# A fused tokenizer, attention and routed-expert kernel: the chunks routed in five groups in place of four

## What is computed

```python
h = h + attn(layernorm(h))      # decayed running sums over the tokens, times mix_w.T, plus mix_b
x = layernorm(h).reshape(-1, 128)
logits = x @ Wg                                  # 8 experts
topw, topi = top_k(logits, 2); topw = softmax(topw)
gu = einsum('nd,edh->enh', x, Wgu) + bgu         # 2 x 256 columns for each expert
eo = einsum('enh,ehd->end', silu(g) * u, Wd) + bd
h = h + sum over the two experts chosen of topw * eo
```

## Time and profile before

| what | before |
|---|---|
| median of 3 runs | 802.29 us (799.72 to 802.66) |
| profiled execution | 798.29 us |
| its span, first to last instruction | 796.5 us |
| busy: PE, POOL, DVE, ACT | 609.1, 475.6, 427.2, 264.0 us |
| mean granted clock of TensorE | 0.825 of 2.4 GHz |
| scatters and gathers (POOL indirect DMAs) | 180 and 180 |
| tiles | 114 |

### The profile page before, as it was taken

How to read it: one execution, slowest core, us unless ns; L and a number is a source line. 1 busy time by engine, 2 the same in 40 slices (tenths; PEclk the granted TensorE clock), 3 DMA queues, 4 the chain that set the end, 5 groups by cost and what they waited for, 6 DMA issues and landing times. The chain is left out here.

```text
span 796.5 us, 12820 instructions
## 1 busy us (share of the span) xinstructions
PE 609.1 (76%) x3335; PEld 521.8 (66%) x3335; DVE 427.2 (54%) x1724; ACT 264.0 (33%) x690; POOL 475.6 (60%) x504
## 2 busy tenths in 40 slices
PE   3692557756998987999989897999898869999000
PEld 2592457755887875788768676888776658887000
DVE  4668787764564565656456664555445323545122
ACT  2611312221533333544324441533433324443000
POOL 5613377634777653566767664677777567750774
PEclk9796557665997877889869987999999979999555
DMA  7197010204565443655646555677767578984221
GB/s 146 44 312 200 2 28 27 78 14 153 171 191 148 144 143 108 199 154 179 192 134 204 150 169 193 180 210 218 218 177 247 155 240 262 279 255 153 75 79 59
DMA packets 84598, 125.23 MB, mean 157 GB/s; under 512 B 15044, under 2 KB 57792, under 8 KB 84526
## 3 DMA queue, kind: packets, MB, share of 16 engines
q1 hardware_dynamic: 72526, 101.66, 42.0%
q0 software_dynamic: 11520, 22.35, 9.9%
q10 hardware_dynamic: 480, 0.41, 0.4%
HBM read 84.25 MB, written 43.25 MB: 160 GB/s over the span
## 5 line engine op out<-in xcount | busy, mean ns | idle before, releaser
L627 PE MATMUL gu<-space,wts 128*128 128x256 f32 x912 | 247.0, 410 | 3.0 <-DVE space L1511 3.0
L1511 DVE SCALAR_TENSOR_TENSOR space<-gu,wts,space 128x256 f32<-128x256 f32 x228 | 108.3, 481 | 237.2 <-ACT space L955 185.5
L1085 POOL DMA_INDIRECT gat<-ybuf,ypos x180 | 177.1, 984 | 94.4 <-issue 56.0
L1071 POOL DMA_INDIRECT xbuf<-x,pos x180 | 183.0, 1017 | 68.2 <-issue 61.8
L955 ACT ACTIVATE space<-gu,wts 128x256 f32<-128x256 f32 x228 | 109.0, 479 | 304.0 <-PE gu L627 303.1
L627 PEld LDWEIGHTS gu<-space,wts 128*128 128x128 f32 x912 | 175.0, 206 | 24.6 <-DVE space L1511 3.8
L627 PEld LDWEIGHTS dn<-wts,space 128*128 128x128 f32 x912 | 126.3, 202 | 21.0 <-DVE space L1511 14.5
L627 PE MATMUL dn<-wts,space 128*128 128x128 f32 x912 | 129.1, 287 | 10.3 <-DVE space L1511 10.3
L1013 POOL TENSOR_TENSOR rs<-ve,nhalf 128x4 f32<-128x4 f32 (+2 forms) x39 | 41.3, 1059 | 73.2 <-DVE ve L1308 48.5
L799 PE MATMUL xTp<-cst,space 128*128 128x128 f32 x228 | 53.3, 319 | 26.0 <-DMA space<-xbuf 26.0
L799 PEld LDWEIGHTS xTp<-cst,space 128*128 128x128 f32 x228 | 26.4, 154 | 42.6 <-DMA space<-xbuf 29.9
(11 more groups left out here) (192 smaller groups left out, 731.7 us busy)
## 6 DMA issues: line engine op xcount, KB each, us to landing
wts<-wall SPq DMA_DIRECT2D x114, 386.0 KB
space<-xbuf SPq DMA_DIRECT2D x114, 128.0 KB, 3.0
ybuf<-space SPq DMA_DIRECT2D x114, 128.0 KB, 2.1
xt<-in_txt_dram SPq DMA_DIRECT2D x16, 256.0 KB, 3.2
xbuf<-zero_rows SPq DMA_DIRECT2D x4, 1024.0 KB, 10.5
xbuf<-zero_rows SPq DMA_DIRECT2D x32, 128.0 KB, 2.2
out_dram<-gat SPq DMA_DIRECT2D x16, 256.0 KB
xbuf<-x,pos POOLq DMA_INDIRECT x180
```

The lines of the kernel that those rows point to most:

```text
L627: return nc.tensor.matmul(o, l, r, start=a, stop=z_)
L1071: nc.gpsimd.indirect_dma_start(out=xbuf, out_offset=bass.IndirectOffsetOnAxis(pos[0:p, c:c + 1], 0), in_=x2[n % NX2][0:p, m // 2 * D:(m // ...
L1085: nc.gpsimd.indirect_dma_start(out=gat[b][0:p, (k * W4 + j) * D:(k * W4 + j + 1) * D], out_offset=None, in_=ybuf[g], in_offset=bass.Indire ...
L1511: V.scalar_tensor_tensor(hid[q % 4], gu_ps[q % 3][:, SLOT:2 * SLOT], wts[k % NW][:, W_B + HT + t:W_B + HT + t + 1], sil[q % 3], ALU.add, A ...
```

## The change

One line. The groups end at chunks 4, 9, 15, 20 and 23 in place of 4, 11, 18 and 23. All that is derived from `GROUPS` follows: the sizes of the buffers, the tile counts, the slots of units, gathers, combines and stores, and the places where a table is made, pads are written and the counting starts anew.

```diff
-GROUPS = [(0, 4), (4, 11), (11, 18), (18, 23)]
+GROUPS = [(0, 4), (4, 9), (9, 15), (15, 20), (20, 23)]
```

## The result

| | before | after |
|---|---|---|
| median of 13 runs each | 798.26 us | 789.94 us |
| profiled execution (span) | 798.29 (796.5) us | 786.35 (784.5) us |
| mean granted clock of TensorE | 0.825 | 0.864 |
| tiles | 114 | 121 |

The ratio is 0.9893, 95% interval [0.9863, 0.9922]: 8.5 us faster (6.2 to 10.9). The forecast was 8.6 us slower. With more runs the median of the kernel before is 798.26; the 802.29 of the forecast came from three of them. One of the 13 runs after (797.47 us) was in a slower state and is left out of the ratio.

What follows compares the result with a forecast made beforehand. It took PE to bound the tile stretches, POOL issuing beside it in dense ones, and POOL's gathers the end. 49.5 - 26.4 - 20.0 + 5.5 + 0 = +8.6 us on 802.29 gave 810.9 us, range 794 to 824.

Steps and rivals of the forecast that it cites:

- Terms 2 and 3: Last group's tiles, 27 become 19: -26.4 us; gathers behind the last tile, 40 become 24: -20.0 us.
- On the SP queue nothing is lost: SP queue: image stores ahead of the boundary at 23 only move, counted at nothing; -4 us if both boundaries were clear.
- Term 1: Tiles ahead of the last group: 87 become 102, the 15 more at PE's own pace of 3.30 us, +49.5 us.
- term 5: What gaps in PE's work and its clock give back or take: 0 us, bounded by -14 and about +12.
- The three sure terms: Tiles ahead of the last group +49.5 us, last group's tiles -26.4 us, gathers behind the last tile -20.0 us.
- Term 4: One more group boundary, where PE drains and waits for rows: +5.5 us, between 2.8 and 8.2.
- The one on the other side (clock): Added tiles fill gaps in intervals 8, 9, 15 to 17; PE stays at 2.4 GHz: -14 us, 796.9 us; chance 0.23.
- POOL: Rival: POOL becomes the bound from interval 16 on, gap term at its upper end, 823 us; chance 0.12.
- The prediction's rule of the highest occupancy: Relieve the busiest engine; that is PE, which the change loads with 23.1 us more: 825 us by the rule alone.

Runs made afterwards that it cites:

- e5: The changed kernel with the first three loads of each group one slot later in SP's order; 0.9979 of before.
- e13: The kernel before with only the last group's first loads two slots earlier; 0.9881 of before.
- e2: The kernel before with five groups ending at 4, 8, 13, 18, 23, so a fifth group without a short last one; 1.0518 of before (837.4 us).
- e7: The kernel before, its four groups kept, with the first three loads of each group two slots earlier; 0.9772 of before.
- e6: The changed kernel with the first three loads of each group two slots earlier; 0.9647 of before (771.8 us).
- e8: The kernel before with four more padded tiles in group 0 (25 in place of 21); 1.0082 of before.
- e10: The kernel before with four more padded tiles in group 2 (39 in place of 35); 1.0127 of before.
- e14: Five groups ending at 4, 8, 13, 18, 23 with the first loads two slots earlier; 1.0291 of before.
- e3: The kernel before with the image chunks' output stores issued from ACT's queue in place of SP's; 1.0198 of before.

## Why the prediction was wrong

- **Terms 2 and 3** (the last group's tiles and gathers) held. The tiles' stretch went from 94.2 to 63.6 us, 30.6 less in place of 26.4, since behind the boundary PE waited 0.82 us for rows in place of 2.14 and the clock did not fall (1.00 against 0.96); what follows them from 60.9 to 41.5, 19.4 less in place of 20.0.
- **The load order, the part's sentence "On the SP queue nothing is lost"**, failed. It looked at which transfers stand on SP and priced the moved image stores at nothing, with -4 us if both boundaries were clear of them. It did not work out at which slot the last half tile falls, and so not that the loads of the last group would pass the drain's stores. Worth 6.9 us by e5, and 9.5 us at the same boundary by e13. The image stores, which the part had in view, are not the cause: e2 and e5 have the wait without them. What this won about pays for the boundary that was added: late loads cost the kernel before some 18 us at its three boundaries (e7 against before) and the changed kernel some 20 us at its three late ones and the small rest (e6 against the change).
- **Term 1 with term 5** (15 tiles at PE's pace, nothing given back) failed by more. With loads early in both, five groups against four are 0.9647 / 0.9772 = 0.987, some 10 us (4 to 16). The three sure terms gave +3.1 and the boundary +5.5. Setting the boundary between 0 and 5.5 leaves 2.4 to 2.0 us for each of the 15 tiles (2.8 to 1.7 with the interval), between the prices that e8 to e10 measured. That is 13 to 19 us less than term 1, where term 5 was taken as 0. A tile behind the last boundary costs its full 3.30; where the others went, they cost very different amounts. Four groups (e7), then five (e6), both with early loads, columns as in the earlier trace rows: intervals 4 to 8; 9 to 17; 18 and 19; from the placing of chunk 20 to the last group's first tile.

```profile
184.32:267.92 83.60, 73.29 (x406) 61.74 (x405) 44.71 (x228) 33.43 (x90) 56.02 (x60) 0.86 0.57 177
267.92:480.87 212.95, 195.85 (x968) 164.35 (x969) 126.84 (x566) 84.90 (x229) 135.50 (x145) 0.84 0.52 160
480.87:538.29 57.42, 56.46 (x329) 48.66 (x327) 32.03 (x127) 25.52 (x71) 39.47 (x43) 1.00 0.77 237
538.29:626.26 87.97, 80.40 (x446) 68.10 (x446) 42.87 (x166) 31.96 (x89) 61.42 (x62) 0.96 0.68 209
```

```profile
182.04:285.86 103.82, 93.27 (x516) 78.88 (x515) 54.99 (x261) 41.44 (x113) 55.68 (x60) 0.88 0.59 179
285.86:505.49 219.63, 201.44 (x1086) 170.43 (x1084) 132.08 (x581) 93.94 (x254) 154.89 (x165) 0.92 0.61 190
505.49:563.19 57.70, 51.17 (x272) 43.11 (x272) 33.87 (x142) 21.33 (x58) 42.76 (x44) 0.91 0.55 170
563.19:664.23 101.04, 97.24 (x562) 83.03 (x561) 48.88 (x182) 40.29 (x114) 70.97 (x73) 1.00 0.78 244
```

Six tiles more in 4 to 8 cost 20.2 us, 3.4 each: PE's own pace. 5.8 more in 9 to 17 cost 6.7 us, 1.2 each, with the clock from 0.84 to 0.92. Six more behind the placing of chunk 20 cost 13.1 us, 2.2 each. (One trace of each kernel; the second stretch holds one boundary in e7 and two in e6, the last one in e6 alone.) The 2.8 tiles that left 18 and 19 gave nothing back, where term 1 has 9.2 us. The forecast had a price between these (1.85 us from 4.4 to 7 tiles) and let it cancel between the intervals that fill and those that empty. It also left interval 10 out of those that become denser; with late loads 10 took 1.3 tiles more in the same 25.3 us.
- **Term 4** (the extra boundary) can't be read apart: its late loads are in the traces at 9, 15 and 20 (waits of 1.5 to 2.7 us), and e6 shows what they cost together with their clock: 0.9647 / 0.9893 = 0.975, some 20 us (15 to 25) for the three and the small rest at 23.
- **The rivals.** The one on the other side (clock) had the right sign, and its mark, a last group ahead of 685, was met. Its price for term 5, -14 us, lies in the 13 to 19 that e6 against e7 leaves, and its mechanism shows in intervals that it named: with late loads, 8, 16 and 17 took 1.2 tiles more each for +0.1, +0.5 and -0.2 us, with the clock from 0.73 to 1.00, 0.93 to 0.93 and 0.86 to 1.00. No run held the clock still, so filled gaps and a higher clock are not told apart. What it did not have is the order of the loads, without which 6.9 of the 8.5 us go. POOL did not set the time as a whole, but in 18 and 19 it is the likely bound: with 5.6 tiles beside it, POOL issues there with one longer wait for another engine, 2.05 us (1.72 in e6), while PE is busy 50.78 of 57.8 us. No run took work from it there. The prediction's rule of the highest occupancy would have given 825; PE did get 13 us busier, and the time fell, since PE's load sat where PE waited anyway.
- **The base.** 4 us of the miss in absolute time are the base: three runs at 802.29, thirteen at 798.26.

Open: why e2 and e14 cost 41 us above four groups. Eight tiles at 1.4 to 3.3 us are 11 to 26. The traces of e14 and e7 put the added time into intervals 4 to 7, at 3.3 us a tile, and 12 to 17, where PE has three waits on DVE of 5.9 to 7.3 us, two of them at tables. No run took these apart.

## What to carry to other kernels

Where work is spread over slots by rounding, work out for each boundary in which slot the last item falls and what stands behind it on every in-order queue: a load that is fixed two slots ahead can stand behind a store that needs everything finished. Price a unit of work by the stretch it goes to, from a run that adds such units there, not by its pace on an engine that is saturated elsewhere; and do not count on the price back where work leaves a stretch. And when a size changes, follow what it does to an order that nobody edited.

## What the runs showed that was not expected

TensorE without rows lost twice: in e5 waits of 4.29 and 1.84 us were followed by eight gate-and-up matmuls in 3.62 us at 1.2 GHz, against 1.89 where the rows were in time. And DMA issue on a compute engine's queue is not free in an in-order program: with the image stores on ACT (e3), issuing four of them took ACT 3.44 us, with the wait ahead of them ACT stood up to 10.95 us before its next instruction, and the kernel lost 2%.
